# A four-stream transformer block: local attention streams rebuilt, copies between streams replaced by numbered homes

## The chip, the cores and the metric

One core of a Trainium2 chip. The time is device microseconds of one execution. Its engines each work through a queue of their own, in order: TensorE (PE) multiplies matrices into the eight PSUM banks, VectorE (DVE), ScalarE (ACT) and GpSimd (POOL) work element by element, SyncE (SP) here issues DMAs. They wait for each other by semaphores only.

## The reference

The input is x of shape (32, 256, 128), float32: 32 sequences of 256 rows. Every sequence goes through the same four steps, and no sequence needs another.

```python
x = x + attention0(layernorm(x))     # 16 heads of 8, softmax over all 256 keys, scale 1/sqrt(128)
x = x + relu(layernorm(x) @ w1 + b1) @ w2 + b2          # 128 -> 512 -> 128
x = x + attention1(layernorm(x)) @ wo.T                 # 16 heads of 8, rotary, causal
x = x + ffn(layernorm(x))            # ffn is itself two layers of the form:
#   h = shift_token(y); q, k, v = split(h @ wqkv)       # 8 heads of 64
#   q, k = l2norm(q) * qs, l2norm(k) * ks; q, k = rotary_xpos(q, k)
#   y = y + local_attention(q, k, v) @ wo               # window of 64, looks one window back
#   h = layernorm(shift_token(y)) * g + b
#   a, g = split(h @ w1 + b1); y = y + (a * gelu(g)) @ w2 + b2
```

shift_token moves the second half of the columns one row down.

## The kernel before

The work of a sequence is cut into four **streams**: ATTN0 (attention 0 and its feed-forward), ATTN1 (attention 1 and the normalised input of the local layers), LOCAL0 and LOCAL1 (one local layer each). A stream is a list of **units** (`attention_units` line 133, `local_units` line 149, `stream_units` line 186): a unit is one step such as `qkv2` or `scores2`, with what it makes each engine do, how many PSUM banks it takes and which semaphores it raises.

The program is a list of **rounds** (`Pass` line 213, `plan` line 232), 37 for 32 sequences. In one round every stream works on another sequence. `TAKES_UP` (line 67) gives the round in which a stream takes up sequence 0, `BEGINS` (line 68) the unit number from which the stream's work belongs to the following round; so a stream's sequence spans two rounds, and in a round come the late units of one sequence and then the early units of the next. The first five rounds (ramp) and the last five (drain) lack some streams. Everything is unrolled. The order of the units in a round is written out by hand for each engine in `TURNS` (line 71): a digit names the stream whose next unit follows. `BANKS` (line 108) gives each use of a bank, in PE's order, one of the eight. A bank may be filled again when its count in `emptied` says so.

The attention streams compute every score twice: once with the keys along the free axis for the row maxima (`maxes`, L1048 to L1059, reduced on DVE in L860), and once transposed with the maxima folded in (`scores`, L1069, exponential on ACT in L696), followed by `mix` (L1088, copied by DVE in L874).

A local layer runs as follows. `shift`: two transposes of Y (L1010), copied to hS by ACT, the lower half one column on (L656, L657). `qkv2` 0 to 5: three products for each of two row tiles (L1124); for q and k ACT squares the bank into rawP (L711) and copies it to rawA (q) or rawB (k) (L713), which gives the bank back, and DVE sums the squares by head (L911). `rope2` 0 to 3 (tile and q or k): POOL multiplies by the cosine table into rawQ (L617), DVE makes the two sine products from rawA or rawB into rawP (L925, L927), POOL adds (L620). `norms2`: DVE clamps the sums (L934), POOL raises them to -1/2 (L625). `scale2`: DVE multiplies back into rawA or rawB (L941). `turn_q2`, `turn_k2`: transposes (L1134), copied by ACT (L679, L684); for K ACT writes rawP, and SP issues two DMAs that put each head's 64 rows into its place in kT2 (L533), since every second head lies on the upper 64 partitions and the rest of kT2 stays zero. `scores2` 0 to 5: mask and scores (L1149 to L1158); 0 and 1 hold query tile 0 for four heads each, 2 to 5 hold query tile 1 for two heads each; DVE takes maxima (L954), ACT exponentials with their sums (L726). `norm2` 0 and 1, by query tile: DVE takes reciprocals (L960) and scales all 8 heads (L964). `turn_p` 0 to 7, one per head: three transposes (L1167 to L1169), copied by ACT (L731); `mix2` 0 to 3 (L1180) for two heads each; `project2` (L1188), added to Y by DVE (L903). `shift_rows`: DMAs on SP move half of the columns one row down (L539). Then `stats`, `apply`, `turn` (ACT, L649), `up2` (L1196, gelu in L736, product on DVE in L970), POOL's `down2` bias (L605), `down2` (L1204, added by DVE in L903). LOCAL1's `finish` adds X and Y on POOL into xout (L631), and SP stores it.

**Handing over.** Each stream has its own home for X, the two local ones for Y as well. Four ACT copies pass values on: ATTN0's result lies in hand01 and ATTN1's `accept` copies it to X1 (L756); ATTN1's `carry` copies X1 to X2 and LOCAL0's `carry` X2 to a half of hand23 (both L748); LOCAL1's `accept` copies both halves of hand23 to XY3 (L762), which must wait for the `finish` of the sequence before. After each of six residual additions DVE waits for its own result and then raises a semaphore (L907).

## Time and profile before

| | us |
|---|---|
| median of 3 runs (3350.9 to 3362.22) | 3358.2 |
| the profiled execution | 3367.69 |
| its span, first to last instruction | 3366.0 |
| PE busy | 3047.4 |
| DVE busy | 2441.8 |
| ACT busy | 2200.7 |
| POOL busy | 1661.0 |
| mean granted clock of TensorE | 0.970 |

Busy time counts the union of the records of an engine; waiting, branching and issuing are not in it. Where an engine was idle, a view names what ended the idle time, taken from the semaphores. The tensor names in the rows are cut: bank stands for all PSUM banks, V, Y, XY, X and hand for the tensors whose names begin so, w_sb and b_sb for weights and biases. Times of a row are microseconds from the start of the span, means are nanoseconds.

### The profile page before, as it was taken

The numbers are of one execution on the slowest core, as the hardware profiler recorded it, in microseconds if no ns is written. First come the engines' busy times: TensorE is split into PE (matmuls) and PEld (weight loads), VectorE is DVE, ScalarE is ACT, GpSimd is POOL, SyncE is SP. The second block draws the span as 40 slices with busy tenths as digits, with TensorE's granted clock in tenths as the row PEclk, the third lists the DMA queues.
The fourth block names the chain that finished last, engine by engine and source line by source line (L and its number), as shares of the span: only waits on it lengthen the run. The fifth ranks groups of instructions, "written<-read, shape, count | busy, mean of one in ns | idle before, by whom it ended". The sixth has DMA issues, their size and how long they took to land.

```text
span 3366.0 us, 61815 instructions
## 1 busy us (share of the span) xinstructions
PE 3047.4 (91%) x20480; PEld 2183.1 (65%) x20480; DVE 2441.8 (73%) x5890; ACT 2200.7 (65%) x6084; POOL 1661.0 (49%) x1741
## 2 busy tenths in 40 slices
PE   4678999999999999999999999999999999988764
PEld 2455776666777766667677766667676766665543
DVE  4355778778777777788777787787777877866543
ACT  2345777767676767676777777676777776765532
POOL 1033555555545455555555555555454555554522
PEclk9789999999999999999999999999999999999877
DMA  2000111111111101111111111111111111110000
GB/s 69 21 18 19 23 24 29 31 30 24 31 25 23 31 23 31 31 24 31 30 26 23 25 29 31 30 25 31 25 23 25 29 31 31 24 23 20 13 15 10
DMA packets 113643, 88.64 MB, mean 26 GB/s; under 512 B 27274, under 2 KB 112692, under 8 KB 113332
## 3 DMA queue, kind: packets, MB, share of 16 engines
q1 hardware_dynamic: 113332, 84.68, 11.1%
q8 instruction: 172, 2.82, 0.3%
q14 instruction: 139, 1.14, 0.1%
HBM read 9.17 MB, written 4.19 MB: 4 GB/s over the span
## 4 chain that ended last, share of the span: by engine, by line
PE 52%; DVE 24%; POOL 10%; issue 5%; ACT 5%; DMA 3%; SPq 1%; DVEq 0%; POOLq 0%; ACTq 0%
DVE negmax L860 10%; POOL rn L625 6%; PE bank L1196 5%; PE bank L1180 5%; PE bank L1069 5%; PE bank L1088 4%; PE bank L1124 4%; PE bank L1134 4%; PE bank L1204 3%; DVE rawA L941 3%; PE bank L1188 3%; PE bank L1016 3%; POOL rawQ L620 2%; PE bank L1158 2%; PE bank L1151 2%
## 5 line engine op out<-in xcount | busy, mean ns | idle before, releaser
L696 ACT ACTIVATE probs<-bank 128x512 f32<-128x512 f32 (+1 forms) x1024 | 478.1, 573 | 205.9 <-PE bank L1069 205.4
L860 DVE TENSOR_REDUCE negmax<-bank 128x2 f32<-128x512 f32 (+1 forms) x896 | 564.8, 682 | 45.3 <-PE bank L1048 27.0
L576 POOL TENSOR_TENSOR veps<-moments,eps_tile 128x2 f32<-128x2 f32 x192 | 37.6, 196 | 938.5 <-DVE moments L809 938.5
L620 POOL TENSOR_TENSOR rawQ<-rawQ,rawP 128x512 f32<-128x512 f32 x256 | 347.4, 1357 | 182.0 <-DVE rawP L927 153.3
L625 POOL TENSOR_TENSOR rn<-ss,minus_half 128x16 f32<-128x16 f32 x128 | 425.1, 3321 | 7.6 <-DVE ss L934 7.5
L1124 PE MATMUL bank<-wqkv_sb,hS 128*128 128x512 f32 x768 | 379.4, 612 | 4.7 <-ACT hS L657 1.7
L1069 PE MATMUL bank<-qT,kT 128*128 128x256 f32 x2048 | 341.6, 301 | 27.7 <-issue 14.0
L1069 PEld LDWEIGHTS bank<-qT,kT 128*128 128x128 f32 x2048 | 278.6, 193 | 98.1 <-ACT qT L679 42.2
L596 POOL TENSOR_SCALAR_AFFINE_SELECT probs<-probs 128x256 f32<-128x256 f32 x512 | 231.5, 480 | 220.4 <-ACT probs L696 217.4
L954 DVE TENSOR_REDUCE negmax<-bank 128x2 f32<-128x384 f32 (+1 forms) x384 | 221.2, 595 | 129.5 <-PE bank L1151 115.5
L1088 PE MATMUL bank<-probs,V 128*16 128x256 f32 (+1 forms) x4096 | 249.7, 358 | 30.1 <-ACT probs L696 27.5
L726 ACT ACTIVATE rawP<-bank,negmax 128x128 f32<-128x128 f32 x512 | 179.7, 375 | 137.0 <-DVE negmax L954 137.0
L1048 PE MATMUL bank<-kT,qT 128*128 128x512 f32 x512 | 194.1, 470 | 33.0 <-DVE negmax L860 22.0
L911 DVE TENSOR_REDUCE ss<-rawP 128x8 f32<-128x512 f32 x256 | 171.3, 680 | 64.9 <-ACT rawP L711 64.6
L726 ACT ACTIVATE P<-bank,negmax 128x192 f32<-128x192 f32 x512 | 210.0, 456 | 4.0 <-DVE negmax L954 3.4
L874 DVE COPY rawC<-bank 128x256 f32<-128x256 f32 x256 | 104.2, 417 | 146.7 <-PE bank L1088 146.7
L1158 PE MATMUL bank<-kT,rawQ 128*128 128x384 f32 x512 | 206.8, 485 | 0.0
L711 ACT ACTIVATE rawP<-bank 128x512 f32<-128x512 f32 x256 | 157.0, 613 | 72.9 <-PE bank L1124 68.4
L1124 PEld LDWEIGHTS bank<-wqkv_sb,hS 128*128 128x128 f32 x768 | 134.5, 195 | 105.4 <-issue 85.3
L679 ACT ACTIVATE qT<-bank 128x512 fp32r<-128x512 f32 x256 | 142.1, 620 | 91.9 <-PE bank L1033 91.9
L617 POOL TENSOR_TENSOR rawQ<-rawB,rope_sb 128x512 f32<-128x512 f32 x128 | 164.3, 1284 | 61.4 <-DVE rawB L941 61.4
L1088 PEld LDWEIGHTS bank<-probs,V 128*16 128x16 f32 x4096 | 91.8, 95 | 158.3 <-issue 61.4
(158 smaller groups left out, 7797.4 us busy)
## 6 DMA issues: line engine op xcount, KB each, us to landing
kT<-rawC SPq DMA_DIRECT2D x256, 128.0 KB, 2.6
kT<-rawP SPq DMA_DIRECT2D x128, 256.0 KB, 3.9
xin<-x SPq DMA_DIRECT2D x32, 128.0 KB, 2.2
out<-xout SPq DMA_DIRECT2D x32, 128.0 KB, 2.2
V<-Y SPq DMA_DIRECT2D x32, 63.5 KB
V<-XY SPq DMA_DIRECT2D x32, 63.5 KB
wqkv_sb<-wqkv SPq DMA_DIRECT2D x1, 1536.0 KB
w_sb<-w SPq DMA_DIRECT2D x1, 682.0 KB
```

What stands on the lines that cost most here:

```text
L596: nc.gpsimd.affine_select(out=part, in_=part, compare_op=ALU.is_ge, fill=0.0, base=0, pattern=[[0, 2], [1, P]], channel_multiplier=-1)\
L620: nc.gpsimd.tensor_tensor(cosine2[:, l, n, :], cosine2[:, l, n, :], two_in_P0[:, l, n, :], ALU.add)\
L625: nc.gpsimd.tensor_tensor(rn[:, l, t].rearrange("p m h -> p (m h)"), ss[:, l, t].rearrange("p m h -> p (m h)"), minus_half[:], ALU.pow).th ...
L696: nc.scalar.activation(dst, src, ACT.Exp, scale=SCALE0 if k == ATTN0 else SCALE1)\
L726: last = nc.scalar.activation(dst, src, ACT.Exp, bias=negmax[:, k, t, hd:hd + 1], accum_out=expsum[:, l, t, hd:hd + 1])
L860: nc.vector.reduce_max(negmax[:, k, t, h0:h0 + nh], tile(u)[:, :].rearrange("p (h k) -> p h k", h=nh), AX.X, negate=True).then_inc(has_emp ...
L954: nc.vector.reduce_max(dst, src, AX.X, negate=True).then_inc(sig("max_done", u), 1)
L1048: last = mm(bank, qT[:, k, g, t * P:(t + 1) * P], kT[:, k, 4 * g + 2 * e:4 * g + 2 * e + 2, :], start=True, stop=True)
L1069: last = mm(tile(u)[:, i * SEQ:(i + 1) * SEQ], kT[:, k, 4 * g + 2 * e + i, t * P:(t + 1) * P], qT[:, k, g, :], start=True, stop=True)
L1088: last = mm(tile(u)[32 * n:32 * n + 16, q0:SEQ], V[:, k, t, 4 * g + n, :], probs[k][t][:, n * w:(n + 1) * w], start=t == 0, stop=t == 1)
L1124: mm(tile(u)[:], hS[:, l, t * P:(t + 1) * P], wqkv2_sb[:, l, m * INNER:(m + 1) * INNER], start=True, stop=True).then_inc(has_filled(u), 1)
L1158: last = mm(two, qT2[:, l, pr, P:SEQ], kT2[:, l, pr, :, WINDOW:SEQ], start=False, stop=True)
```

## The change

Values no longer move: X of a sequence has one of five homes XB, chosen by the sequence number modulo 5, Y one of three homes YB. `carry` and `accept` are gone. Who writes a new value into a home waits for the output of the sequence five or three before. The six additions raise the bank's own count alone, and those who need the sum wait for that count; LOCAL1's `shift` waits for LOCAL0's `down2` of the same sequence.

In the local streams, `qkv2` of q and k now lets ACT square the bank into a part of P1 (two strips of 64 columns per head), copy it to rawA or rawB, and raise raw_ready; DVE sums the squares and then makes the two sine products straight from the bank, into rawQ (q) or rawP (k), and gives the bank back. `rope2` is split: `cos2` (POOL, in place in rawA or rawB) and `add2` (POOL, in place); `scale2` works in place too. `turn_k2`: ACT writes kT2 itself, two copies of 64 partitions each, and SP's DMAs are gone. `scores2` comes in the order 0, 2, 3, 1, 4, 5, and `norm2` goes by halves of the heads: half 0 needs `scores2` 0, 2, 3, and `turn_p` 0 to 3 wait for half 0 only, 4 to 7 for half 1. The small one of the two row-shift DMAs is issued first. The memsets on POOL at the start come in another order.

`BEGINS`, all five lists of `TURNS` and `BANKS` are new. The units of a round number 166 on PE as before, with the same matmuls.

```diff
-BEGINS = (33, 39, 29, 16)
+BEGINS = (21, 33, 25, 8)
...
 TURNS = {
     "tensor": (
-        "22200200222222333333122111120100003333331102222000"
-        "01222103333320330332233331111111311300002220011011"
-        "22333320003330031111111100003331131133311131100010"
-        "12222222222222200003001111100000220222210001110010"
-        "002233333333"
+        "20002220223311111333333222220002222222000022103333"
+        "33333211100100333331000001130102222001233303303230"
+        "02333331111133122000032220012220222222221111333330"
+        "00330011311110011331011013333331112222222110100010"
+        "0022200010111103"
...
-    units += [rope(0), norms(0), rope(1), scale(0), rope(2), norms(1), scale(1), rope(3), scale(2), scale(3)]
+    units += [qkv(0), cosine(0), qkv(1), cosine(1), norms(0), qkv(3), add(0), scale(0), qkv(4), add(1), scale(1),
+              cosine(2), cosine(3), qkv(2), qkv(5), norms(1), add(2), scale(2), add(3), scale(3)]
     units += [Unit("turn_q2", u, bank=1) for u in range(2)]
-    units += [Unit("turn_k2", u, bank=1, k_in=2 * 16 * u) for u in range(2)]
-    units += [Unit("scores2", u, bank=1, max_done=1) for u in range(6)]
-    units += [Unit("norm2", t, rec_done=1, p_ready=1) for t in range(TT)]
+    units += [Unit("turn_k2", u, bank=1) for u in range(2)]
+    units += [Unit("scores2", u, bank=1, max_done=1) for u in (0, 2, 3, 1, 4, 5)]
+    units += [Unit("norm2", half, rec_done=1, p_ready=1) for half in range(2)]
...
-        X1 = sb("X1", [P, TT, DIM])
-        X2 = sb("X2", [P, TT, DIM])
-        Y2 = sb("Y2", [P, TT, DIM])
-        XY3 = sb("XY3", [P, 2, TT, DIM])
-
-        hand01 = sb("hand01", [P, TT, DIM])
-        hand23 = sb("hand23", [P, 2, TT, DIM])
+        XB = sb("XB", [P, KEPT_X, TT, DIM])
+        YB = sb("YB", [P, KEPT_Y, TT, DIM])
...
-                    for e in range(2):
-                        half = slice(64 * e, 64 * e + 64)
-                        sp.dma_start(kT2[half, l, :, e, :], two_in_P0[half, l].rearrange("p u (g q) -> p (u g) q", g=2))\
-                            .then_inc(sig("k_in", u), 16)
...
+                elif u.kind == "turn_k2":
+                    act.wait_ge(has_filled(u), uses(u))
+                    for e in range(2):
+                        half = slice(64 * e, 64 * e + 64)
+                        last = nc.scalar.activation(kT2[half, l, 2 * u.part:2 * u.part + 2, e, :],
+                                                    tile(u)[half].rearrange("p (a q) -> p a q", a=2), ACT.Copy)
+                    last.then_inc(has_emptied(u), 1)
...
-                        nc.scalar.activation(two_in_P0[:, l, m, :], tile(u)[:], ACT.Square).then_inc(sig("sq_ready", u), 1)
+                        nc.scalar.activation(squares[m][:, l], tile(u)[:].rearrange("p (h d) -> p h d", h=HEADS), ACT.Square)\
+                            .then_inc(sig("sq_ready", u), 1)
                     dst = (q2, k2, V2)[m]
-                    nc.scalar.activation(dst[:, l, t, :], tile(u)[:], ACT.Copy).then_inc(has_emptied(u), 1)
+                    nc.scalar.activation(dst[:, l, t, :], tile(u)[:], ACT.Copy)\
+                        .then_inc(sig("raw_ready", u) if m < 2 else has_emptied(u), 1)
...
-                    for sem, count in newest(pas, j, taken(u, 0)):
-                        dve.wait_ge(sem, count)
-                    dve.sem_inc(sig("handed" if u.kind == "down0" else "resid", u), 1)
                 elif u.kind == "qkv2" and u.part % 3 < 2:
                     t, m = u.part // 3, u.part % 3
-                    dve.wait_ge(sig("sq_ready", u), so_far("sq_ready", k, u, pas, j) + 1)
-                    nc.vector.reduce_sum(ss[:, l, t, m, :], two_in_P0[:, l, m, :].rearrange("p (h d) -> p h d", h=HEADS),
-                                         AX.X).then_inc(sig("sums", u), 1)
+                    dve.wait_ge(sig("sq_ready", u), so_far("sq_ready", u) + 1)
+                    nc.vector.reduce_sum(ss[:, l, t, m, :], squares[m][:, l], AX.X).then_inc(sig("sums", u), 1)
+                    dve.wait_ge(sig("raw_ready", u), so_far("raw_ready", u) + 1)
+                    raw = tile(u)[:].rearrange("p (h d) -> p h d", h=HEADS)
                     tab = rope2_sb[:, l, t, m, 1, :]
-                    sn = two_in_P0[:, l, n, :].rearrange("p (h d) -> p h d", h=HEADS)
+                    sn = sines[m][:, l, t, :].rearrange("p (h d) -> p h d", h=HEADS)
...
-                        .then_inc(sig("sin_part", u), 1)
+                        .then_inc(has_emptied(u), 1)
...
-                    part = P0[:, l] if t == 0 else P1[:, l, :, WINDOW:SEQ]
-                    n = P if t == 0 else SEQ - WINDOW
-                    nc.vector.tensor_tensor(part, part, recip[:, k, t, 0:HEADS].unsqueeze(2).broadcast_to([P, HEADS, n]),
-                                            ALU.mult).then_inc(sig("p_ready", u), 1)
+                    for t, part, n in ((0, P0[:, l, own], P), (1, P1[:, l, own, WINDOW:SEQ], SEQ - WINDOW)):
+                        last = nc.vector.tensor_tensor(part, part, recip[:, k, t, own].unsqueeze(2).broadcast_to([P, 4, n]), ALU.mult)
+                    last.then_inc(sig("p_ready", u), 1)
```

## Rows read from the trace of the kernel before

**Rows 1.** The page, section 1: busy time, share of span, instructions per engine

```profile
PE 3047.4 (91%) x20480; PEld 2183.1 (65%) x20480; DVE 2441.8 (73%) x5890; ACT 2200.7 (65%) x6084; POOL 1661.0 (49%) x1741
```

**Rows 2.** Busy time by stretch: bounds, length, each engine, clock, DMA share, GB/s

```profile
359.60:2938.10 2578.50, 2493.29 (x17284) 1799.35 (x17280) 2024.75 (x4941) 1846.09 (x5131) 1396.67 (x1459) 1.00 0.12 27
...
3031.50:3126.20 94.70, 78.04 (x464) 54.50 (x464) 60.84 (x137) 54.82 (x156) 49.16 (x50) 0.93 0.10 20
3126.20:3220.40 94.20, 67.43 (x355) 46.58 (x355) 53.06 (x103) 45.24 (x130) 43.61 (x38) 0.85 0.07 15
```

**Rows 3.** Timeline of PE in one full round: start, duration (us), instruction

```profile
1661.38 0.40 PE L1053 MATMUL bank<-kT,qT 128*128 128x512 f32 x1
1661.62 0.39 PE L1057 MATMUL bank<-kT,qT 128*128 128x512 f32 x1
```

**Rows 4.** Waits of PE in the full rounds: total us, times, longest

```profile
PE bank L1088 <- ACT probs L696: 18.9, 54, 0.4
PE bank L1048 <- DVE negmax L860: 15.1, 27, 0.9
...
PE bank L1033 <- DVE negmax L860: 8.7, 26, 0.4
PE bank L1149 <- DMA kT<-rawP: 7.0, 8, 1.3
PE bank L1069 <- DVE rawC L874: 5.8, 19, 0.6
```

**Rows 5.** Single lines of ACT: durations ns min/median/max, first and last start

```profile
L656 ACT ACTIVATE hS<-bank x64: 365/373/379, 204.8 to 3282.4; 64x256 f32<-64x256 f32 x64
L684 ACT ACTIVATE rawP<-bank x128: 592/605/620, 247.9 to 3314.3; 128x512 f32<-128x512 f32 x128
```

**Rows 6.** The chain that ended last, in the drain: start us, us, what

```profile
3016.39 3.96 DMA kT<-rawP
...
3314.26 0.61 ACT rawP L684
...
3315.67 3.92 DMA kT<-rawP
3319.63 0.80 PE bank L1149
```

**Rows 7.** Timeline of all engines in the last local layer

```profile
3322.90 0.37 ACT L726 ACTIVATE rawP<-bank,negmax 128x128 f32<-128x128 f32 x1 [6.74 <-DVE negmax L954]
...
3329.18 0.48 ACT L726 ACTIVATE P<-bank,negmax 128x192 f32<-128x192 f32 x1
...
3331.93 0.48 PE L1167 MATMUL bank<-ident_r,rawP 128*128 128x128 f32 x1 [4.09 <-DVE P L964]
```

**Rows 8.** DVE's scaling of probabilities, durations as in rows 5

```profile
L964 DVE TENSOR_TENSOR rawP<-rawP,recip x64: 1224/1225/1800, 263.2 to 3328.6; 128x1024 f32<-128x1024 f32 x64
L964 DVE TENSOR_TENSOR P<-P,recip x64: 1757/1759/2252, 265.0 to 3330.1; 128x1536 f32<-128x1536 f32 x64
```

**Rows 9.** Groups by line and form: busy us, mean ns, idle before, releasers

```profile
L925 DVE TENSOR_TENSOR rawP<-rawB,rope_sb 128x256 f32<-128x256 f32 x128 | 87.8, 686 | 0.0
...
L927 DVE TENSOR_TENSOR rawP<-rawA,rope_sb 128x256 f32<-128x256 f32 x128 | 56.6, 442 | 0.0
```

**Rows 10.** DVE products, durations as in rows 5; the second reads a bank

```profile
L925 DVE TENSOR_TENSOR rawP<-rawB,rope_sb x128: 408/422/1464, 225.6 to 3306.2; 128x256 f32<-128x256 f32 x128
...
L836 DVE TENSOR_TENSOR rawC<-bank,rope_sb x64: 389/418/425, 138.5 to 3074.1; 128x256 f32<-128x256 f32 x64
```

**Rows 11.** Groups of POOL, columns as in rows 9

```profile
L625 POOL TENSOR_TENSOR rn<-ss,minus_half 128x16 f32<-128x16 f32 x128 | 425.1, 3321 | 7.6 <-DVE ss L934 7.5
L620 POOL TENSOR_TENSOR rawQ<-rawQ,rawP 128x512 f32<-128x512 f32 x256 | 347.4, 1357 | 182.0 <-DVE rawP L927 153.3 <-ACT rawP L684 23.5
```

**Rows 12.** Groups of ACT, columns as in rows 9

```profile
L762 ACT ACTIVATE XY<-hand 128x512 f32<-128x512 f32 x32 | 20.3, 634 | 96.0 <-POOL xout L631 96.0
L756 ACT ACTIVATE X<-hand 128x256 f32<-128x256 f32 x32 | 13.4, 418 | 73.0 <-DVE Y L824 73.0
```

More of the change, by code:

```diff
@@ L463, in run, with newest @@
[L463 to L472 removed]
+        def newest(*counts):
+            return [(emptied[c[1]], max(n for b, n in counts if b == c)) for c in dict(counts)]
```

551 lines of the change are left out of this document (246 added, 305 removed).

## The prediction

> **What bounds the kernel now.** I read the page of the profile first. PE is busy 91% of the span, DVE 73%, ACT 65%, POOL 49% [rows 1]: no engine but PE is near full. Then the busy time by stretch [rows 2]. The 37 rounds fall into a ramp (up to 359.6 us), 27 full rounds in which all four streams run (359.6 to 2938.1, that is 2578.5 / 27 = 95.5 us each, clock 1.00) and five drain rounds. PE's records are busy 2493.29 of the 2578.5 us, so it shows 85.2 us of idle there, 3.2 us per round. Those records overlap: two matmuls of 128x512 start 0.24 us apart while each is recorded as 0.40 us [rows 3]. A gap shorter than about 0.16 us behind a matmul is therefore invisible, and PE can be later than 3.2 us per round without showing it.
>
> The drain says what else is near the limit. Its second and third rounds still take 94.7 and 94.2 us although PE's busy time falls to 78.0 and 67.4 us [rows 2]. ATTN0 has ended by then, and the length stays nearly what it was. So beside PE's work there is a second limit of nearly the same length: the chain of one local layer (square sums, rotation, K to its place, scores, softmax, projection, row shift, feed-forward), which runs once per round in LOCAL0 and in LOCAL1, coupled by the in-order queues. Both limits are close together in a full round, so shortening the second frees only part of the first.
>
> Last, who keeps PE waiting in the full rounds [rows 4]: DVE's maxima 15.1 + 8.7 us, its copy to rawC 5.8 us and the DMA of the local K 7.0 us, together 36.6 us; exponentials on ACT 18.9 us. The matmuls themselves are the same after the change.
>
> **Part 1: the local K without a DMA.** Today two copies on ACT (0.61 us, 128x512 [rows 5]) put K into rawP, SP waits for them and issues two transfers, and the first scores wait. In the last layer the second copy begins at 3314.26, the transfer takes 3.92 us from 3315.67 on, and PE starts at 3319.63 [rows 6]. The change writes kT2 from ACT: four copies of 64 partitions in place of two of 128. A 64x256 copy takes 0.37 us [rows 5], so halving the partitions saves little; I take 0.6 us for 64x512 (bounds 0.37, and 0.62, the slowest copy of the full shape [rows 5]). The first part ends 0.6 us later than today and the second takes 1.2 us, so K is ready at 3314.26 + 0.6 + 1.2 = 3316.1 and the scores start some 3.6 us earlier. ACT pays 4 x 0.6 = 2.4 us per round more. This transfer is five times on the chain of the drain, first at 3016.39 and last at 3315.67 [rows 6], and once in the ramp. SP, which stood at this wait, comes sooner to what is queued behind it, above all the row shift and the output.
>
> **Part 2: softmax in two halves.** The exponentials of the last layer run from 3322.90 to 3329.18 + 0.48 = 3329.66 and the first transpose of the probabilities starts at 3331.93, PE having idled 4.09 us [rows 7]. After the change the first four heads, both query tiles, are done after half of 6.8 us, at 3326.3. DVE's two multiplications take 1.225 us for 1024 and 1.759 us for 1536 elements [rows 8], that is 1.04 ns per element and 0.16 us fixed. Halves cost 512 x 1.04 + 160 = 0.69 us and 768 x 1.04 + 160 = 0.96 us, and with 0.2 us for the reciprocal (an estimate, a little above the fixed part) 1.85 us. The first transpose can start at 3328.2, 3.7 us earlier, and the second half (ready 3329.7 + 1.85 = 3331.5) hides under the transposes and mixing of the first. DVE pays two more multiplications and no more reciprocals per layer, 2 x 0.16 x 2 = 0.6 us per round. On the chain of the drain such a multiplication stands five times, of which four feed the transposes, the last at 3330.1 [rows 8].
>
> **Part 3: rotation.** DVE's sine products read two SBUF operands today. They come in four forms of 128, recorded with means from 442 to 686 ns [rows 9], 286.3 us in all, with a median of 0.42 us and a longest of 1.46 us [rows 10]. The same shape read from a bank takes 0.42 us without spread (389 to 425 ns, the other row of [rows 10]). The change reads the bank, so I take 512 x 0.42 = 215 us: 71 us less on DVE, 2.2 us per round. (Upper bound of the price: as today, nothing gained.) The long ones lie beside POOL's products. SBUF — State Buffer (section "SBUF: two separate sides") of the Trainium skill says that a VectorE instruction with two SBUF inputs and a GpSimd instruction that reads SBUF exclude each other through one shared port pair. By that rule the excess of these 512 goes; by a plain reading of the medians it could return on another instruction that collides instead, since scale2 still has two SBUF inputs; the sum takes its term from PE's waits and is the same by both. POOL's own instructions stay: the sum 1.36 us, the cosine at most the same, the norm 3.32 us [rows 11], 8 x 1.36 + 2 x 3.32 = 17.5 us per layer. Its sums now stand 153.3 us in all behind the sine products [rows 11], 153.3 / 64 = 2.4 us per layer; the cosines and sines can be made ahead, so I take 2 us off the layer's chain (bounds 0 and 2.4), three times in the drain. The price: the bank of each q and k part is now given back by DVE after its two products, not by ACT after its copy. Square sum and copy run side by side, so that is 2 x 0.42 = 0.84 us longer, for 8 of the 166 bank uses of a round. In the new list at least 2.5 us of PE work (an estimate, from start distances like those of [rows 3]) stand between such a use and the next fill, beside 1.6 us at the least today, so I cost it at nothing; it has a price if DVE comes late (below).
>
> **Part 4: copies and counts between streams.** Four ACT copies go, three of 128x256 at 0.42 us or just under and one of 128x512 at 0.63 us, 1.9 us per round, and ACT's waits in front of two of them, 96.0 and 73.0 us in all, 5.3 us per round [rows 12]. With the 2.4 us of part 1 ACT's work rises by 0.5 us per round, at 1846.09 of 2578.5 us busy [rows 2] not a limit. Of the waits only the head-of-line part counts: work behind them on ACT (exponentials, transposed probabilities) is released. Where ACT finds nothing else ready, nothing is gained. DVE's wait for its own result after six residual additions goes as well (an estimate of 0.2 us each, like the fixed part above, 1.2 us per round), and I cost the replacement, a wait on the bank's own count, at nothing. The new waits, on the output of the sequence three or five back, were satisfied two rounds earlier; they hold nothing.
>
> **Part 5: order.** All five queues and the banks are in a new order, and the streams change rounds at units 21, 33, 25 and 8. A round has the same PE work. The new order leaves 2.8 and 3.7 us of PE work (by today's start distances) between last K transpose and first scores, where 5.1 and 7.3 us were left for the transfer; elsewhere the distances are similar, some shorter (LOCAL1's normalised turn directly before its first up-projection). No row shows this order, so it is the wide part: from nothing at all to all 85.2 us of visible idle, or beyond zero on the other side.
>
> **The sum.** Full rounds: the edits relieve DVE (2.2 + 1.2 - 0.6 = 2.8 us per round) and the K transfer, so I take away the 36.6 us of PE waits that name these two, 1.4 us per round. Drain: 5 x 3.6 + 4 x 3.7 + 3 x 2 = 39 us off the chain, of which I count two thirds, 26, because PE is still busy most of its early rounds and the two local layers hide each other in part. Ramp: one transfer, one softmax, with the same two thirds, rounded up for a copy, 6 us. Together 69 us. The profiled execution ran 3367.7 us (span 3366.0), 9.5 above the median of the runs, so it becomes 3299; the median 3358.2 becomes 3289.
>
> **Rivals.** (a) The full rounds gain much more: the local chain was what really held the 95.5 us, and all visible idle goes: 85 + 39 + 9 = 133 us, 3225. For it: drain rounds of the same length with half the work. Against it: 18.9 us of PE's waits are for ACT's exponentials, which are unchanged. A rule speaks for more room as well: Perfetto Trace Analysis (section "Identifying the Most-Contended Engine") of the Trainium skill says that matmul busy time is no good measure of a full TensorE; the overlapping records agree, and the weight loads are busy 65% [rows 1].
> (b) Only ramp and drain gain, because in a full round PE was the limit and a new wait takes each old one's place: 26 + 6 = 32 us, 3326.
> (c) Nothing measurable: the new order loses 1.2 us per round and 27 x 1.2 = 32 us eat the rest, 3358.
> (d) Slower: q and k parts hold their DVE unit and their bank for the sines. DVE is in order; each of the 8 now puts 0.84 us of products right behind the square sum, ahead of maxima and copies that PE waits for. At 8 x 0.84 = 6.7 us per round that PE could see in full, it decides against the change from 1.2 us per round on. If a third lands on PE, 2.2 us per round, 59 us less the 32: 3385.
> That the change does not do what it says I leave out: copies and transfers are plainly gone.
>
> **Chances and range.** Forecast 0.38 (3255 to 3315), (a) 0.17, (b) 0.17, (c) 0.09, (d) 0.19. Faster by over 0.3% is 0.72, within 0.3% (10 us, about what a measurement tells from no change) 0.09, slower 0.19. The range 3205 to 3385 reaches over (a) by the error of its drain and up to (d); what is left out is the worse half of (d) and a steady round shorter by over 4 us.
>
> **What would show it.** No transfer from rawP and no copies in the profile; sine products at 0.42 us from bank; full rounds of 94.1 us; drain shorter by some 26 us; first transposed probabilities soon after the first half of the exponentials. Wrong if the period stays at 95.5 or rises, and if PE then waits for DVE in front of maxima (d), or if the drain keeps 94 us rounds, which would say that the order and not the chain's length set them.

## The result and the profile after

The changed kernel takes 3203.79 us (median of 4 runs, 3203.11 to 3205.84), the kernel before 3356.4 in the same comparison: ratio 0.9544 [0.953, 0.9558]. The forecast was 3289 with a range of 3205 to 3385: right in direction, less than half of the gain, and just outside its range. The profiled executions stand at spans of 3366.0 and 3201.4 us, 164.6 apart, and this is split here, each stretch beginning with the first PE work of a round:

| stretch | before | after | forecast | measured |
|---|---|---|---|---|
| ramp | 359.6 | 326.0 | -6 | -33.6 |
| 27 full rounds | 2578.5 (95.5 each) | 2488.7 (92.2 each) | -36.6 | -89.8 |
| five drain rounds | 427.9 | 386.7 | -26 | -41.2 |

The page of after: busy time of each engine, and the shares of the chain that ended last, by engine.

```profile
PE 2938.8 (92%) x20480; PEld 2173.0 (68%) x20480; DVE 2391.8 (75%) x6018; ACT 2236.8 (70%) x6084; POOL 1561.3 (49%) x1741
...
PE 60%; DVE 19%; ACT 8%; POOL 5%; issue 3%; DMA 2%; SPq 1%; DVEq 0%; POOLq 0%; ACTq 0%
```

The same chain line on the page of the kernel before, which the prediction did not use:

```profile
PE 52%; DVE 24%; POOL 10%; issue 5%; ACT 5%; DMA 3%; SPq 1%; DVEq 0%; POOLq 0%; ACTq 0%
```

Half of the chain of before ran through other engines although PE was recorded busy for 97% of the full rounds. That line pointed away from PE's work as the limit; e11 below shows it.

Busy time by stretch of after (bounds, length, then PE, weight loads, DVE, ACT, POOL, granted clock of PE, DMA share, GB/s), the full rounds and drain rounds 2 to 4:

```profile
326.00:2814.70 2488.70, 2416.92 (x17282) 1806.85 (x17281) 1991.93 (x5050) 1880.15 (x5131) 1308.34 (x1458) 1.00 0.08 17
...
2908.60:2991.30 82.70, 70.71 (x466) 50.22 (x465) 57.01 (x141) 54.59 (x158) 46.79 (x49) 1.00 0.05 11
2991.30:3067.80 76.50, 60.22 (x381) 41.88 (x379) 47.45 (x108) 46.20 (x139) 43.72 (x42) 0.94 0.02 4
3067.80:3136.80 69.00, 51.21 (x270) 37.30 (x271) 30.42 (x68) 32.47 (x106) 13.90 (x15) 0.85 0.02 5
```

Against [rows 2]: PE's visible idle in the full rounds went from 85.2 to 71.8 us, only 13.4 less. Its recorded busy time fell by 76.4 us with the same matmuls (17284 and 17282 records). So five sixths of the gain came out of time that was recorded as busy, and the clock is no cause of it: it was granted at 1.00 in both. The prediction had named this (a pause shorter than the tail of a record does not show) but took its term from visible waits all the same.

Who keeps PE waiting in the full rounds of after:

```profile
PE bank L933 <- DVE V L766: 30.3, 27, 1.1
PE bank L1119 <- ACT rawQ L603: 17.7, 27, 0.7
PE bank L992 <- ACT qT L633: 4.9, 18, 0.3
PE bank L939 <- DVE rawP L851: 4.7, 21, 0.2
```

All of [rows 4] is gone, the 18.9 us behind ACT's exponentials too. The two largest waits in their place belong together, the turn and the first up-projection of the last local layer (48.0 us in all).

Single lines of DVE, ACT and POOL after (ns min/median/max, first and last start):

```profile
L849 DVE TENSOR_TENSOR rawQ<-bank,rope_sb x128: 406/415/417, 207.9 to 3139.5; 128x256 f32<-128x256 f32 x128
L887 DVE TENSOR_TENSOR rawP<-rawP,recip x128: 691/692/983, 250.0 to 3169.4; 128x512 f32<-128x512 f32 x128
L887 DVE TENSOR_TENSOR P<-P,recip x128: 944/950/1154, 250.6 to 3170.0; 128x768 f32<-128x768 f32 x128
L859 DVE TENSOR_SCALAR ss<-ss x128: 156/168/1243, 210.1 to 3147.8; 128x16 f32<-128x16 f32 x128
L642 ACT ACTIVATE kT<-bank x256: 578/592/596, 239.5 to 3158.7; 64x512 f32<-64x512 f32 x128
L579 POOL TENSOR_TENSOR rn<-ss,minus_half x128: 2911/2912/2915, 212.5 to 3148.0; 128x16 f32<-128x16 f32 x128
```

### The profile page after: what moved, and what is told of

It is laid out like the page before. It is cut to its first block, busy times and chain, and to the rows that moved or that the text cites. A ratio compares the mean times of both kernels' runs of the same rounds, so it can differ in the third digit from the quotient of the medians.

```text
span 3201.4 us, 60855 instructions
## 1 busy us (share of the span) xinstructions
PE 2938.8 (92%) x20480; PEld 2173.0 (68%) x20480; DVE 2391.8 (75%) x6018; ACT 2236.8 (70%) x6084; POOL 1561.3 (49%) x1741
## 4 chain that ended last, share of the span: by engine, by line
PE 60%; DVE 19%; ACT 8%; POOL 5%; issue 3%; DMA 2%; SPq 1%; DVEq 0%; POOLq 0%; ACTq 0%
PE bank L992 7%; PE bank L1011 7%; DVE negmax L802 5%; PE bank L1103 5%; PE bank L1080 5%; PE bank L1119 4%; PE bank L1047 4%; PE bank L1073 3%; PE bank L971 3%; DVE ss L844 3%; POOL rn L579 3%; ACT kT L642 2%; PE bank L1090 2%; PE bank L1058 2%; PE bank L956 2%
## 5 line engine op out<-in xcount | busy, mean ns | idle before, releaser
L802 DVE TENSOR_REDUCE negmax<-bank 128x2 f32<-128x512 f32 (+1 forms) x896 | 552.7, 678 | 31.2 <-PE bank L971 28.8
L656 ACT ACTIVATE probs<-bank 128x512 f32<-128x512 f32 (+1 forms) x1024 | 497.0, 571 | 44.3 <-PE bank L992 37.7
L579 POOL TENSOR_TENSOR rn<-ss,minus_half 128x16 f32<-128x16 f32 x128 | 372.7, 2912 | 150.4 <-DVE ss L859 150.0
L546 POOL TENSOR_SCALAR_AFFINE_SELECT probs<-probs 128x256 f32<-128x256 f32 x512 | 210.9, 438 | 349.3 <-ACT probs L656 345.9
L567 POOL TENSOR_TENSOR rawA<-rawA,rope_sb 128x512 f32<-128x512 f32 x128 | 176.1, 1376 | 148.1 <-ACT rawA L675 148.1
L1011 PE MATMUL bank<-probs,V 128*16 128x256 f32 (+1 forms) x4096 | 237.4, 357 | 7.2 <-ACT probs L656 6.7
L1119 PE MATMUL bank<-rawQ,w_sb 128*128 128x256 f32 (+1 forms) x768 | 214.4, 414 | 21.6 <-ACT rawQ L603 21.6
L567 POOL TENSOR_TENSOR rawB<-rawB,rope_sb 128x512 f32<-128x512 f32 x128 | 170.1, 1329 | 113.1 <-ACT rawB L675 113.1
L672 ACT ACTIVATE P<-bank 128x512 f32<-128x512 f32 x256 | 154.9, 605 | 56.4 <-PE bank L1047 55.2
L844 DVE TENSOR_REDUCE ss<-P 128x8 f32<-128x512 f32 x256 | 173.5, 678 | 26.4 <-ACT P L672 26.4
```

The costliest lines, as they stand in the source:

```text
L567: nc.gpsimd.tensor_tensor(raw, raw, tab, ALU.mult).then_inc(sig("cos_part", u), 1)
L579: nc.gpsimd.tensor_tensor(rn[:, l, t].rearrange("p m h -> p (m h)"), ss[:, l, t].rearrange("p m h -> p (m h)"), minus_half[:], ALU.pow).th ...
L656: nc.scalar.activation(dst, src, ACT.Exp, scale=SCALE0 if k == ATTN0 else SCALE1)\
L802: nc.vector.reduce_max(negmax[:, k, t, h0:h0 + nh], tile(u)[:, :].rearrange("p (h k) -> p h k", h=nh), AX.X, negate=True).then_inc(has_emp ...
L844: nc.vector.reduce_sum(ss[:, l, t, m, :], squares[m][:, l], AX.X).then_inc(sig("sums", u), 1)
L1011: last = mm(tile(u)[32 * n:32 * n + 16, q0:SEQ], V[:, k, t, 4 * g + n, :], probs[k][t][:, n * w:(n + 1) * w], start=t == 0, stop=t == 1)
```

## The experiments

Each run is set against the kernel before, measured beside it on the same chip; the medians of before in these comparisons lie between 3356.4 and 3362.67 us. "New edits" are the changed operations, "new order" the TURNS, BEGINS and BANKS of after. The question was which of the two brings the 3.3 us a round, and what a round is bound by. This table gives the stretches of each profiled execution, cut as above, and the clock that PE was granted in the full rounds. Single executions of before spread from 3350.9 to 3371.24 us, up to 0.75 us a round, so a few tenths of a us a round between two profiles of the old order tell nothing.

| run | order | ratio, 95% | ramp | full round | drain | clock |
|---|---|---|---|---|---|---|
| before | old | 1 | 359.6 | 95.5 | 427.8 | 1.00 |
| after | new | 0.9544 [0.953, 0.9558] | 326.0 | 92.2 | 386.7 | 1.00 |
| e1 all edits | old | 1.0926 [1.0906, 1.0945] | 360.2 | 107.1 | 414.6 | 0.96 |
| e5 edits, bank given back early | old | 1.0521 [1.0504, 1.0539] | 357.2 | 102.5 | 405.5 | 1.00 |
| e13 edits, old rotation | old | 1.0213 [1.0195, 1.0232] | 358.7 | 98.8 | 407.3 | 1.00 |
| e6 K from ACT only | old | 1.0039 [1.0025, 1.0053] | 356.5 | 95.9 | 421.6 | 1.00 |
| e7 softmax halves only | old | 0.9993 [0.9984, 1.0002] | 358.0 | 95.2 | 426.8 | 1.00 |
| e2 four operations undone | new | 1.1937 [1.1911, 1.1963] | 342.8 | 118.0 | 474.7 | 0.93 |
| e3 K by DMA | new | 1.0153 [1.0131, 1.0174] | 331.1 | 98.5 | 421.3 | 0.97 |
| e15 the same, LOCAL0 only | new | 0.9903 [0.9885, 0.992] | 331.9 | 96.0 | 402.2 | 0.98 |
| e14 the same, LOCAL1 only | new | 0.987 [0.9855, 0.9886] | 323.9 | 95.6 | 406.9 | 0.97 |
| e4 softmax by tile | new | 1.0157 [1.0138, 1.0175] | 328.4 | 99.1 | 407.6 | 0.98 |
| e8 copies back | new | 0.9956 [0.9942, 0.9971] | 325.5 | 96.7 | 403.3 | 0.98 |
| e9 sines from SBUF, bank early | new | 1.0094 [1.0068, 1.012] | 325.6 | 99.0 | 392.9 | 0.97 |
| e10 sines from SBUF, bank held | new | 1.0265 [1.0238, 1.0292] | 337.5 | 100.7 | 398.0 | 0.96 |
| e16 one exchange on PE | new | 0.9575 [0.9557, 0.9594] | 329.0 | 92.7 | 385.9 | 0.99 |
| e11 masks out | old | 0.9978 [0.9963, 0.9994] | 353.5 | 95.2 | 426.2 | 1.00 |
| e12 masks out | new | 0.951 [0.9481, 0.9539] | 325.9 | 92.2 | 377.2 | 0.99 |

The clock has to be read with every length here. In before, after, e5, e13, e6, e7 and e11 PE had its full clock in nearly all of the full rounds. In the others it did not, as around one wait for the transfer in e3 (a stretch that ends with the wait, one that follows soon after, and the first matmul behind the wait):

```profile
1539.16:1543.48 4.32, 2.16 (x19) 1.96 (x17) 0.76 (x2) 3.60 (x8) 1.53 (x4) 1.00 0.55 127
1544.51:1547.93 3.42, 3.42 (x9) 2.23 (x7) 1.45 (x4) 2.10 (x11) 0.00 (x0) 0.50 0.04 9
...
1543.48 0.51 PE L1077 MATMUL bank<-masks,ident_r 128*128 128x512 f32 x1 [2.16 <-DMA kT<-rawP]
```

PE had stood idle for 2.16 us, and soon after it ran at half clock (0.50, the lower of its two levels, 1.2 instead of 2.4 GHz) without being idle. Such time is recorded as busy. One minus the granted clock, times the length of a round, estimates what a round lost by it, at most, as not all of it need lie on the critical path: 0.4 us in after, 2.9 in e3, 2.4 in e14, 2.0 in e15, 2.3 in e4 and in e8, 3.4 in e9, 4.2 in e10, 1.3 in e12, 0.6 in e16, 4.1 in e1, 0.5 in e5, 8.7 in e2.

### Edits and order apart

e1 keeps the edits and takes the order of before, unit for unit on PE:

```diff
-BEGINS = (21, 33, 25, 8)
+BEGINS = (33, 38, 33, 19)
```

TURNS and BANKS change with it (not shown).

> The kernel after, with its edits (K straight from ScalarE, softmax halves by heads, sine products from the bank, no copies, three and five homes) but the order of work and the banks of the kernel before: TensorE's order of units is that of before, unit for unit. Theory A (the edits take the waits away, the order only follows): about 3210 to 3230 us, ratio 0.957 to 0.963. Theory B (the new order and its head start do it, the edits nothing): 3340 to 3360, ratio 0.995 to 1.0. Theory C (the edits shorten the local stream, and only an order laid out for the shorter stream uses it): between, 3290 to 3330, ratio 0.98 to 0.992.

e2 keeps the new order and undoes together what e3, e4, e8 and e10 below undo one by one. It is not the whole old form: the homes and the split rotation stay, and the bank is still held until the sine products are made, as it never was before. Its output differs.

> The order of after, with the old forms of the operations put back in it: K by copy and DMA, softmax by tile, sine products from SBUF (not from the bank; the values there are not the rotated ones, so the output differs), and the four hand-over copies as copies of the same size onto a spare strip, with the wait of VectorE behind each addition. Theory A: back to about 3330 to 3360 (0.992 to 1.0). Theory B: 3205 to 3225 (0.955 to 0.961). Theory C: 3260 to 3310 (0.972 to 0.986), the drain alone worse by 5 x 3.6 + 4 x 3.7 = 33 us.

Measured: 3671.8 and 4013.58 us, outside every number expected. Neither half brings a part of the gain: each by itself makes the kernel slower, by 9% and by 19%, and the clock (at most 4.1 and 8.7 us a round) explains only a part of the 11.6 and 22.5 us by which their rounds exceed those of before. The additions that write the output show the distance of the rounds (the first and the last of n outputs between 600 and 2500 us, so the length is their difference over n - 1); before, after, e1, e2:

```profile
L631 POOL TENSOR_TENSOR xout<-XY x20: 724/732/735, 609.8 to 2425.0; 128x256 f32<-128x256 f32 x20
...
L585 POOL TENSOR_TENSOR xout<-XB,YB x20: 724/730/737, 682.4 to 2433.1; 128x256 f32<-128x256 f32 x20
...
L566 POOL TENSOR_TENSOR xout<-XB,YB x18: 727/730/742, 637.9 to 2460.6; 128x256 f32<-128x256 f32 x18
...
L596 POOL TENSOR_TENSOR xout<-XB,YB x16: 722/725/731, 673.5 to 2441.7; 128x256 f32<-128x256 f32 x16
```

That is 95.5, 92.1, 107.2 and 117.9 us. The ramp divides more simply: the old order with the new edits starts its full rounds at 360.2 us, as before; the new order with the old forms at 342.8 and with the new edits at 326.0. The ramp's gain needs the new order, and half of it came with the order alone, the other half only with the edits in it.

### Why the edits are slower in the old order

PE's waits of e1 between 500 and 2600 us:

```profile
PE bank L937 <- DVE rawP L832: 74.4, 20, 4.0
PE bank L973 <- DVE rawP L832: 26.4, 20, 1.5
```

L832 is the second sine product, which gives the qkv2 bank back; L937 and L973 are attention work that needs the bank. e5 gives the bank back from ACT again; the sine products then read a strip of weights in SBUF, so its output differs:

```diff
-                        .then_inc(sig("raw_ready", u) if m < 2 else has_emptied(u), 1)
+                        .then_inc(has_emptied(u), 1)
...
-                    raw = tile(u)[:].rearrange("p (h d) -> p h d", h=HEADS)
+                    raw = wqkv2_sb[:, l, 0:INNER].rearrange("p (h d) -> p h d", h=HEADS)
```

> As the kernel with the new edits in the old order (3672 us, 107.4 us a round), but ScalarE gives the qkv2 bank back with its raw copy, as before, and the sine products read SBUF again (a weight strip that nothing writes, so the output differs) and run 0.94 us each. Theory bank hold: TensorE's waits there that name the sine products (L937 and L973, 100.8 us in 20 rounds, 5 us a round) are for the bank that they hold, so they go: 102 us a round or less, 3525 us or less (ratio under 1.05). Theory of the queue place: the sine products stand in front of other work of VectorE, and twice as long they stall more: 107 us a round or more, ratio 1.09 or more.

Measured 3532.89 us and 102.5 us a round, just above the numbers of the held bank (3525 and 102) and far from those of the queue place: the hold costs 4.6 us a round in the old order, although the longest products went from 0.42 to 1.49 us. Up to 3.6 of the 4.6 us can be the clock, which fell to 0.96 in e1 with waits of up to 4.0 us and is back at 1.00 in e5. PE then waits for maxima:

```profile
PE bank L955 <- DVE negmax L784: 62.9, 41, 1.8
```

e13 also moves the sine products back to their old place in DVE's queue (its output differs too):

```diff
+                elif u.kind in ("cos2", "add2") and u.part in (0, 2):
+                    t, m = u.part // 2, 0 if u.kind == "cos2" else 1
+                    u = earlier(u, "qkv2", 3 * t + m)
```

> The new edits in the old order, but the rotation of the local layers as before: the bank given back by ScalarE, the sine products (0.94 us, from a weight strip, so the output differs) at the place in VectorE's queue where before has them. What is left of the change is K straight from ScalarE, the softmax by halves, no copies and three and five homes. If the early place of the sine products in VectorE's queue is what costs the run with the bank free (3533 us, 102.5 us a round, TensorE waiting for maxima): back to 3340 to 3375 (0.994 to 1.005). If the homes and the missing copies cost (waits for an older sequence): still 3450 or more. If the copies' going is worth what the prediction gave it: 3320 or less.

Measured 3434.66 us: between the numbers of two theories. The early place in the queue costs another 3.7 us a round. The two together, 8.3 us, are rival (d) of the prediction, queue place and bank, at nearly four times its price, in the old order. What is left, 98.8 against 95.5 us, is more than K from ACT (e6) and the softmax by halves (e7) cost by themselves; which of POOL's in-place products, the homes or their waits it is was not tried.

e6 and e7 put one edit each into the kernel before. e6 is the turn_k2 hunk of the change with its wait; e7 is:

```diff
-    units += [Unit("scores2", u, bank=1, max_done=1) for u in range(6)]
+    units += [Unit("scores2", u, bank=1, max_done=1) for u in (0, 2, 3, 1, 4, 5)]
...
-                    if u.part == 0:
-                        pe.wait_ge(sig("p_ready", u), so_far("p_ready", k, u, pas, j))
+                    if u.part % 4 == 0:
+                        made = earlier(pas, u, "norm2", u.part // 4)
+                        pe.wait_ge(sig("p_ready", made), so_far("p_ready", k, made, pas, j) + 1)
```

> The kernel before, with one edit: ScalarE puts the turned local K straight into its place, the copy and the two DMAs go. Theory of the sum: the 7.0 us of its full rounds and 5 x 3.6 us of the drain go, 3335 us (0.9925). Theory of the fitted order: the order of before leaves 5 to 7 us of TensorE's work between K and the scores, so full rounds gain nothing and only the drain does, 3342 (0.9945) or less; ScalarE's two longer copies may cost up to 0.3 us a round, 3350.

> The kernel before, with one edit: the softmax of the local layers is scaled by halves of the heads, the scores are taken 0, 2, 3, 1, 4, 5, and the turned probabilities of heads 0 to 3 wait for the first half only. Theory of the sum: 4 x 3.7 us in the drain, 3345 us (0.9955). Theory of the fitted order: the full rounds are no shorter, as the order has its other streams' work there, and any change of place costs: 3345 to 3400.

Measured 3370.58 and 3356.54 us, with 3359.25 for the kernel before beside them; the second cannot be told from no change. The transfer's going is worth less than nothing in the old order: the 7.0 us of PE's waits for it are not worth their length, and the kernel is 11 us slower. In the profiles the round grew by 0.4 us (ACT's longer copies may be that, which was not tried), and the drain gains 6.2 us instead of 18.

### What each edit is worth in the new order

e3, e4, e8, e9 and e10 undo one thing each in the kernel after. e3 also places SP's unit for LOCAL1's K at the head of SP's queue in a round (e2, e14 and e15 too); the units moved with it give SP nothing else to do.

```diff
-                    for e in range(2):
-                        half = slice(64 * e, 64 * e + 64)
-                        last = nc.scalar.activation(kT2[half, l, 2 * u.part:2 * u.part + 2, e, :],
-                                                    tile(u)[half].rearrange("p (a q) -> p a q", a=2), ACT.Copy)
-                    last.then_inc(has_emptied(u), 1)
+                    nc.scalar.activation(two_in_P0[:, l, u.part, :], tile(u)[:], ACT.Copy).then_inc(has_emptied(u), 1)
...
+                        sp.dma_start(kT2[half, l, :, e, :], two_in_P0[half, l].rearrange("p u (g q) -> p (u g) q", g=2))\
+                            .then_inc(sig("k_in", u), 16)
```

> The kernel after, with the local K again copied whole by ScalarE and spread by two DMAs of SyncE's queue before the scores. Theory A: the DMA was the end of 7.0 us of waits in full rounds and of five drain rounds at 3.6 us, so 25 us of the gain go: about 3229 (0.962). Theory B (order alone): under 5 us, 3204 to 3209. Theory C: in the new order the DMA is met in every round (the turned K stands 2.8 to 3.7 us of TensorE's work ahead of the first scores where it stood 5.1 to 7.3 before), so 1 to 2 us in each of 27 rounds and 3.6 us in each of five: 3249 to 3276 (0.968 to 0.976).

e4 is the softmax hunk of the change backwards:

> The kernel after, with the local softmax scaled by tile, all 8 heads of a tile at once, and the scores taken in the order 0 to 5, so that the first turned probabilities wait for all six. Theory A: about 4 x 3.7 = 15 us in the drain and 5 in the full rounds, 3220 to 3225 (0.959 to 0.961). Theory B: 3204 to 3209. Theory C: 2 us in each full round more, as TensorE's next piece of that stream stands right behind it: 3260 to 3280 (0.971 to 0.977).

e8 puts copies of the old sizes back on ACT, and DVE's wait behind each addition:

```diff
+                elif u.kind == "apply" and u.source == "z":
+                    act.wait_ge(sig("passed_on", u), so_far("passed_on", u) + 1)
+                    copy_aside()
+                    copy_aside()
+                elif u.kind == "down2" and k == LOCAL0:
+                    copy_aside()
+                elif u.kind == "finish":
+                    act.wait_ge(sig("out_ready", u), so_far("out_ready", u) + 1)
+                    for e in range(2):
+                        copy_aside()
...
+                    for sem, count in newest(taken(u)):
+                        dve.wait_ge(sem, count)
```

> The kernel after, with copies of the size of the four hand-overs on ScalarE again (onto a spare strip; the longest of them as two), each behind a wait for its source, and VectorE's wait behind each addition. Some 5 x 0.45 us of ScalarE in a round. If the gain came from the copies' going as one term among others: 10 us, 3214 (0.9575). If the new order is fitted to the durations, each round grows by 1 us or more as with the other two undone edits: 3235 to 3400 (0.964 to 1.013). If copies are free: 3204.

e9 is e5's edit in the new order; e10 only has the sine products read the strip of squares. The output of both differs.

> The kernel after in its own order, but the qkv2 bank is given back by ScalarE's raw copy and the sine products read SBUF (a weight strip, so the output differs), 0.94 us each in place of 0.41, 8 pairs a round, about 4 us of VectorE a round more. Fitted order: as the other undone edits, 2 to 6 us a round, 3260 to 3400 (0.97 to 1.01), and TensorE's new waits name VectorE. If the bank hold is what costs in the new order too: 3204 or less.

> The kernel after, the bank still held until the sine products are made, but these read SBUF (the strip of squares, so the output differs) at 0.94 us each. Against the run with the bank given back early it tells the price of the hold in the new order: fitted order, hold hidden: the two within 0.5%. Hold not hidden: this one slower by 3 us a round or more, over 80 us.

Measured 3414.86, 3413.59, 3343.01, 3394.99 and 3452.64 us. Each undone edit costs 139 to 249 us, which is most of the gain or more than all of it. The losses add: those of e3, e4, e8 and e10 make 809 us together, and e2, which undoes all four at once, lost 810; their rounds are longer by 26.3 us added up and by 25.8 in e2. So in the new order none of the four hides behind another. At most 1.9 to 3.9 us a round of each are the clock (over the 0.4 of after). PE's waits between 500 and 2600 us in e3, e4, e8 and e9:

```profile
PE bank L1077 <- DMA kT<-rawP: 94.1, 43, 2.8
...
PE bank L1091 <- DVE P L888: 100.4, 42, 2.8
...
PE bank L1069 <- ACT hS L620: 55.3, 43, 2.4
...
PE bank L936 <- DVE probs L767: 60.5, 21, 2.9
```

In e3 and e4 the wait stands right where the edit was undone, once per local layer and round: there the new order has PE arrive just when the shortened operation is done. In e8 PE waits for the copy of `shift` (hS), which stands behind the copies in ACT's queue. In e9 it waits for the normalisation of ATTN0 (L767), whose mean is 1.20 us there and 0.60 in the full rounds of after. e9 and e10 differ by 58 us, and their sine products take the same time (399 and 400 us in all). What differs is the bank's hold and that ACT must wait for the strip of squares until it is read (72 us of its waits in e10); the two are not told apart, so the price of the hold in the new order stays open.

### What a round is made of

A circle of waits is a chain in which every instruction waits for the one before, and which leads from a piece of work in one round to the same piece in the next; its length is then the length of the round. e14 and e15 undo K in one local layer only.

> The kernel after with the K copy and DMA undone in the second local layer alone (both layers: 98.8 us a round against 92.2, 3415 us). If one circle of waits runs through both layers, each delay is paid in turn: half, 95.5 us a round, about 3300 (0.983). If each layer is bound by a circle of its own, one delay costs as much as two: 98 us a round, over 3380.

> The same for the first local layer alone. One circle through both layers: 95.5 us a round, about 3300, and the two halves add up to the 6.6 us of both. Circles of their own: 98 us for at least one of the two, and the sum of both halves over 6.6.

Measured 3318.27 and 3328.59 us: rounds of 95.6 and 96.0 us, 3.4 and 3.9 more than after, and 6.3 more for both together (e3). Less the estimate for the clock this is 1.4, 2.3 and 3.8 us. The delays of the two layers are paid one after the other, as the theory of one circle through both layers has it; which instructions make up the circle was not followed. PE's waits for the transfer are only 42.6 us in 22 rounds (e14), 1.9 a round:

```profile
PE bank L1087 <- DMA kT<-rawP: 42.6, 22, 2.3
```

The loss is 3.4. The rest does not show as idle time: PE's recorded busy time rose by 1.7 us a round (2463.0 us in the 27 rounds, 2416.9 in after), and the clock, 0.97, accounts for up to 2.0.

e11 and e12 take the masks' matmuls out of the local scores, in before and in after (the output differs).

```diff
-                        mm(bank, ident_r[:], band0.unsqueeze(1).broadcast_to([P, 4, P]), start=True, stop=False)
...
-                        mm(two, ident_r[:], band1.unsqueeze(1).broadcast_to([P, 2, SEQ - WINDOW]), start=True, stop=False)
```

> The kernel before without the 12 matmuls a round that add the masks to the local scores (so the softmax there runs over unmasked scores and the output differs): TensorE is lighter by about 2.3 us a round. If TensorE's own work bounds a round of 95.5: 2 to 2.5 us a round less, about 3280 to 3290 (0.977 to 0.98). If a chain through several engines bounds it, with TensorE's work on it only in part: under 1 us a round, 3330 to 3358.

> The kernel after without the same 12 matmuls (output differs). TensorE as the bound of the 92.2 us round: 3130 to 3145 (0.932 to 0.937). Chain: 3180 to 3204 (0.947 to 0.954). If the order is fitted so closely that any change of durations disturbs it: not less, 3200 or more.

Measured 3354.01 us (0.9978 [0.9963, 0.9994]) and 3197.74 (0.951 [0.9481, 0.9539]). Busy time of e11 in the window of [rows 2], and the outputs of e12 between 600 and 2500 us:

```profile
359.60:2938.10 2578.50, 2459.93 (x17060) 1742.76 (x17060) 2030.85 (x4949) 1850.32 (x5139) 1390.99 (x1465) 1.00 0.12 28
...
L585 POOL TENSOR_TENSOR xout<-XB,YB x20: 722/727/736, 682.9 to 2433.6; 128x256 f32<-128x256 f32 x20
```

PE is busy 33.4 us less than in [rows 2] although the window holds a little more than 27 rounds of e11. Its own 27 rounds take 2570.2 us with PE busy 2451.6: 41.7 us less work, of which 33.4 became idle time and 8.3 came off the rounds. The clock is 1.00 in both, so PE's work is not the bound of a full round in before. In after, the round with 12 matmuls less is 92.1 us as with them. That says the same less cleanly, since the clock fell from 0.996 to 0.986 in e12 and can have taken back up to 0.9 us a round.

e16 tries to fill one visible wait of PE. The order of its units:

```
after: ... turn/LOCAL1, up2 0/LOCAL1, turn/ATTN0 (h), up2 1/LOCAL1 ...
e16:   ... turn/LOCAL1, turn/ATTN0 (h), up2 0/LOCAL1, up2 1/LOCAL1 ...
```

> The kernel after with one exchange in TensorE's order: the turn of stream 0 (0.44 us) goes between the turn of the last local layer and its first up matmuls, where TensorE now waits 0.66 us a round for ScalarE's copy; the banks go with their work. If a wait of TensorE is worth its length: 0.3 to 0.45 us a round, about 3192 (0.951). If the round is a circle through other engines: up to 0.2 us a round, 3198 to 3204, or slower where the later up matmuls stand on it.

Measured 3217.01 us, 13 us slower than after (10 by the two ratios, whose intervals just touch). PE in one round of after and of e16:

```profile
1497.53 0.44 PE L933 MATMUL bank<-ident_r,V 128*128 128x128 f32 x2 [1.11 <-DVE V L766]
1498.63 1.13 PE L1119 MATMUL bank<-rawQ,w_sb 128*128 128x256 f32 x4 [0.66 <-ACT rawQ L603]
1499.84 0.44 PE L933 MATMUL bank<-ident_r,probs 128*128 128x128 f32 x2
...
1506.66 0.44 PE L933 MATMUL bank<-ident_r,V 128*128 128x128 f32 x2 [1.11 <-DVE V L766]
1508.96 0.69 PE L933 MATMUL bank<-ident_r,probs 128*128 128x128 f32 x2 [1.86 <-DVE probs L766]
```

The turn that was moved up was not ready: a wait of 0.66 us became one of 1.86, and the round grew by 0.6 us in the profile.

## Why the prediction was right and wrong

**What bounds the kernel.** It saw two limits, PE's work and the local chain, and took PE as the first. PE's work is not it (e11; e12 less cleanly). Delays in the two local layers are paid in sequence (e3, e14, e15), and so are those of four operations (e2), as in a circle of waits through all of them. The prediction's own clue pointed there, drain rounds of the same length with half the work; it took the chain of one layer for a second limit behind PE.

**Full rounds, -36.6 against -89.8: the step that failed.** It priced the edits by PE's waits that name DVE and the transfer, 1.4 us a round, and the order at nothing. The round became 3.3 us shorter. PE's waits are no measure in either direction. The 7.0 us for the transfer were worth nothing in the old order (e6), and the transfer costs 6.3 us a round in the new one (e3). Rival (a), 85 us off the full rounds because the local chain holds them, came within 5 us of this stretch, though not by the idle that it named, of which 71.8 us are still there. It was held back by the 18.9 us of waits behind exponentials; these went too, by the new order, with the exponentials unchanged.

**Ramp, -6 against -33.6.** The term counted edits. They bring nothing measurable in the old order (360.2 us in e1). The order had no term: it brings 16.8 us alone and 33.6 with the edits in it.

**Drain, -26 against -41.2.** For K the size is right at the last layer. From the first K copy to the first scores were to be 2.4 us: the first copy begins at 3156.87 and the scores at 3159.43, 2.56. For the rotation it was far too small. The prediction took 2 us off a layer's chain, at most 2.4. In the last layer the first product of `qkv2` begins at 3283.20 before and at 3134.15 after, the first transpose of q at 3310.55 and 3154.01: 27.4 us became 19.9, 7.5 less. The new order is not needed for most of it (22.2 us in e13, 21.8 in e1, both in the old order), and the sine products from the bank are not either (e13 has the old ones). The split rotation in place is common to all three; it was not undone by itself. For the softmax the term was too large. From the first exponential to the first transposed probability 9.03 us in [rows 7] became 7.35, so 1.7 us were saved and not 3.7. DVE in the last layer of after:

```profile
3165.21 1.38 DVE L878 TENSOR_REDUCE negmax<-bank 128x4 f32<-128x512 f32 x2 [0.54 <-PE bank L1073]
3166.85 0.56 DVE L878 TENSOR_REDUCE negmax<-bank 128x2 f32<-128x384 f32 x1 [0.26 <-PE bank L1080]
3167.33 0.19 DVE L884 RECIPROCAL recip<-expsum 128x8 f32<-128x8 f32 x1
3167.56 0.69 DVE L887 TENSOR_TENSOR rawP<-rawP,recip 128x512 f32<-128x512 f32 x1
3168.16 0.95 DVE L887 TENSOR_TENSOR P<-P,recip 128x768 f32<-128x768 f32 x1
```

The first half stands behind the maxima of the second in DVE's queue. In the old order K alone gives the drain 6.2 us (e6), the softmax 1.0 (e7), all edits with the old sine products 20.5 (e13), and all edits 13.2 (e1). The new order without the four operations makes it 46.9 us longer (e2), so the 41.2 need both. That the second to fourth drain round become shorter one after the other (82.7, 76.5, 69.0) and no longer stay at 94 needs no new order: in e1 they are 99.5, 83.4 and 80.1 us.

**Durations, right but for one.** Sine products from the bank 0.415 us without spread (0.42 forecast), kT2 copies 0.592 (0.6), scaling 0.692 and 0.950 (0.69 and 0.96). POOL's norm was taken over at 3.32 us and came out at 2.91 without spread, 0.8 us less on each layer's chain; it is 2.91 in e1 and e2 as well, so neither the order nor the four operations make it so. Of DVE's 2.8 us a round, 1.2 were waits behind the additions, which are no busy time; the busy time was to fall by 1.6 us a round and fell by 1.2 (2024.75 to 1991.93). The sine products fell from 230.6 to 178.4 us in the full rounds, but the clamp L859 grew from 17.9 to 46.6 us, the first scaling of q from 101.4 to 107.9, and ATTN0's first normalisation from 16.3 to 30.5, together 49.4 of the 52.2 us: it returned on other instructions, as the open end on collisions allowed. This is the shared port of SBUF — State Buffer (section "SBUF: two separate sides") of the Trainium skill as far as the sine products go: with an operand in a bank the spread is gone. The clamp has one SBUF input and still reached 1.24 us. The same section also names an instruction in a two-port mode; no run here tells whether the clamp is one.

**Rival (d)** is real, 8.3 us a round in the old order (e1, e5, e13); how much of it is left in the new one no run tells. The prediction priced it at 2.2 and gave it 0.19. By the edits that the sum counted, with the order at nothing, the kernel would be 9% slower (e1). That the forecast direction held is owed to the order, about which it had said that no row shows it: as far as the sum goes, luck.

**The range** ended at 3205. It left out "a steady round shorter by over 4 us", but the round was shorter by 3.3 only, close to the 85 us of rival (a). What went past the range lies in ramp and drain, 74.8 us together, where (a) had 48 and the sum 32.

## What to carry to other kernels

In a kernel whose rounds overlap and whose queues are laid out by hand, read the shares of the chain that ended last beside the busy times and the waits: when half of it lies off an engine that is recorded 97% busy, try whether that engine's work is the bound at all, as e11 does, before pricing edits by its waits. An order and the durations that it was laid out for are one change; the price of an edit taken alone in the old order (here nothing measurable for one, 11 us lost for another, 237 lost for the early sine products from the held bank) says nothing of its price in the new one (here 139 to 249 us). Where runs of different clock are compared, read the granted clock of the stretch before the idle time. If a change brings a new order with it, the time between the neighbours of each shortened operation, added up through both layers, seems the thing to work out, and a range should reach to its full length; no run here tried a forecast made this way.

## What was not expected of the hardware

PE's recorded busy time is not fixed by its matmuls: 17284 records cover 2493.3 us before and 17282 cover 2416.9 after, at a granted clock of 1.00 in both. A wait cost PE more than its length where the clock fell behind it: in e3 idle time grew by 4.0 us a round over after and busy time, with the same matmuls, by 2.3. The sine products show the cost of two SBUF operands most plainly: 0.404 to 0.418 us with one in a bank, up to 1.49 us for the same shape from SBUF (e10):

```profile
L852 DVE TENSOR_TENSOR rawQ<-P,rope_sb x128: 408/944/1492, 211.8 to 3393.8; 128x256 f32<-128x256 f32 x128
```
